# Graph network kernel: the destination tiles of the two convolutions cut into chunks of 2, 3, 3, 3, 3, 3, 4, 4 instead of 1, 3, 3, 3, 3, 4, 4, 4

## The reference

```
xw   = x @ W
norm = rsqrt(deg[src]) * rsqrt(deg[dst])
h    = segment_sum(xw[src] * norm, dst) + b
# first network: batch norm over the nodes, relu, h = x + h
# second: layer norm over the features, silu, then a two-head attention
```

## Time and profile before

| | us |
|---|---|
| median of three runs | 3359.72 |
| lowest, highest | 3355.37, 3362.70 |
| profiled execution, own time | 3363.56 |
| its span, first to last instruction | 3361.9 |
| first convolution, first to last matmul | 298.1 to 379.8 |
| second convolution, first matmul to last sums copied | 419.0 to 515.6 |

### The profile page before, as it was taken

The page is one execution under the profiler, slowest core; times in us unless marked ns, Lnnn a source line. Parts: engine busy times, 40 slices in busy tenths (PEclk is TensorE's granted clock), DMA queues, the critical chain, the costliest instruction groups (busy, mean ns, idle before and its releaser), DMA issues. The chain is left out here.

```text
span 3361.9 us, 41194 instructions
## 1 busy us (share of the span) xinstructions
PE 2803.2 (83%) x13998; PEld 2153.0 (64%) x13998; DVE 1752.6 (52%) x4008; ACT 1368.4 (41%) x2596; POOL 965.7 (29%) x786
## 2 busy tenths in 40 slices
PE   6778797999996999999999999999744455447997
PEld 3446684777774778778887877786433344435775
DVE  8997657999977351121111112112544443356994
ACT  4573134999996121111111111111413333342896
POOL 6110070000000643223222322220177777740000
PEclk9998897999998999999999999999855555555999
DMA  4434352111002432212121212210242221113200
GB/s 151 144 105 157 137 200 88 40 40 77 8 1 92 162 117 88 79 59 98 59 94 68 88 64 98 85 64 5 87 129 47 46 55 29 29 19 128 79 35 20
DMA packets 79695, 266.66 MB, mean 79 GB/s; under 512 B 21129, under 2 KB 53344, under 8 KB 70176
## 3 DMA queue, kind: packets, MB, share of 16 engines
q1 hardware_dynamic: 62520, 236.50, 18.9%
q0 software_dynamic: 16976, 27.54, 3.8%
HBM read 232.80 MB, written 31.18 MB: 79 GB/s over the span
## 5 line engine op out<-in xcount | busy, mean ns | idle before, releaser
L2798 PE MATMUL psum<-gate_stream,parts 128*128 128x384 f32 (+1 forms) x3600 | 668.8, 344 | 15.9 <-POOL gate_stream L2871 11.6
L2798 PEld LDWEIGHTS psum<-gate_stream,parts 128*128 128x128 f32 x3600 | 632.4, 189 | 32.9 <-issue 13.4
L2871 POOL CAST gate_stream<-gate_adj 128x1920 fp32r<-128x1920 f16 (+1 forms) x200 | 370.6, 1860 | 851.9 <-PE psum L2798 829.7
L2150 PE MATMUL psum<-gat_h,gat_pair 128*128 128x129 f32 (+1 forms) x3750 | 571.9, 292 | 8.6 <-DVE gat_pair L1954 7.8
L2150 PEld LDWEIGHTS psum<-gat_h,gat_pair 128*128 128x128 f32 (+1 forms) x3750 | 462.4, 191 | 123.3 <-issue 77.9
L1482 POOL DMA_INDIRECT edge_rows<-edge_table,src_idx x440 | 429.8, 977 | 181.4 <-issue 133.8
L2889 DVE SCALAR_TENSOR_TENSOR gate_work<-psum,bhh,gate_work 128x384 f32<-128x384 f32 (+1 forms) x80 | 50.0, 626 | 793.7 <-PE psum L2761 763.1
L1954 DVE SCALAR_TENSOR_TENSOR gat_pair<-gat_above,gat_adj 128x512 f32<-128x512 f32 (+3 forms) x525 | 326.4, 622 | 87.7 <-PE psum L2150 58.7
L2063 ACT ACTIVATE gat_above<-psum,gat_as 128x512 f32<-128x512 f32 (+3 forms) x525 | 329.4, 627 | 42.7 <-PE psum L2138 41.0
L2054 ACT ACTIVATE psum<-gat_ad_rows,gat_as 128x512 f32<-128x512 f32 (+3 forms) x525 | 334.9, 638 | 16.8
L1909 DVE SCALAR_TENSOR_TENSOR gat_acc<-gat_adj,gat_q,gat_acc 128x512 f32<-128x512 f16 (+3 forms) x497 | 328.3, 677 | 0.0
(11 more groups left out here) (484 smaller groups left out, 3700.1 us busy)
## 6 DMA issues: line engine op xcount, KB each, us to landing
gate_adj<-adj SPq DMA_DIRECT2D x35, 2400.0 KB, 8.1
gat_adj<-adj SPq DMA_DIRECT2D x8, 3200.0 KB, 10.8
adj<-count_stage SPq DMA_DIRECT2D x196, 100.0 KB, 1.7
gcn_adj<-adj SPq DMA_DIRECT2D x8, 2400.0 KB, 8.1
edge_place<-row_scratch SPq DMA_DIRECT2D x40, 352.0 KB, 3.6
gate_adj<-adj SPq DMA_DIRECT2D x5, 2800.0 KB, 9.0
gcn_adj<-adj SPq DMA_DIRECT2D x4, 3200.0 KB, 10.0
edge_rows<-edge_table,src_idx POOLq DMA_INDIRECT x440
```

The costliest lines, as they stand in the source:

```text
L2150: mm = e.matmul(ps[0:p, b, a:a + D + 1], pair[:, g % 2, i * P:i * P + p], h1[:, hi, h, :], start=hi == 0 and i % 3 == 0, stop=hi == NT - 1 ...
L2798: mm = e.matmul(ps[:, f, 0:hi - lo], parts[:, t, m, f, :], stream[:, (NGG * i + t // GG) % GR, 0:windows(i), t % GG * W:(t % GG + 1) * W], ...
L2871: e.tensor_copy(stream[:, n % GR, 0:windows(i), :], cols[:, i % 2, 0:windows(i), g * GW:(g + 1) * GW]).then_inc(widened, 1)
```

## The change

The list of tiles is changed, and with it the table that says at which of the last counting steps VectorE adds the identities of chunks 0 and 1, which are now five tiles in place of four. The chunk widths go from 128, 384, 384, 384, 384, 512, 512, 448 to 256, 384, 384, 384, 384, 384, 512, 448.

```diff
-GCN_TILES = (1, 3, 3, 3, 3, 4, 4, 4)
+GCN_TILES = (2, 3, 3, 3, 3, 3, 4, 4)
...
-        own_at = {BSTEPS - 1: (0, 0), BSTEPS - 2: (1, 0), BSTEPS - 3: (1, 1), BSTEPS - 4: (1, 2)}
+        own_at = {BSTEPS - 1: (0, 1), BSTEPS - 2: (0, 0), BSTEPS - 3: (1, 2), BSTEPS - 4: (1, 1), BSTEPS - 5: (1, 0)}
```

## The result

The kernel with chunks of 2, 3, 3, 3, 3, 3, 4, 4 took 3353.64 us (median of 18 runs, 3347.85 to 3363.21), and the kernel before, run beside it, 3358.61 (18 runs, 3353.5 to 3364.2). The ratio is 0.9985, with a 95% interval of 0.9978 to 0.9992: 5.0 us shorter, between 2.7 and 7.4. The profiled execution took 3350.91 us, span 3349.3, mean granted clock 0.875 (before 0.87).

The account below looks back on a forecast made before the run. The prediction took TensorE to bound the first convolution and a loop over four engines the second, from chunk 2 on. Terms of -2.4 and -1.5 us sum to -3.9, forecasting 3356.0 us, range 3351.5 to 3361.5.

Parts of the forecast that it names:

- "same" by the bound of 0.2%: Whole kernel: a change within about 0.2% (6.7 us) counts as no change; chance 0.79, faster 0.17, slower 0.04.
- Chunk 5: First convolution: 384 columns in place of 512 at full clock, 11.67 to 8.76 us, 2.91 us gained.
- Chunk 0 and the clock: First convolution: chunk 0 of 256 columns 0.3 us longer at 11.25; clock rises 0.33 us later, at 313.85.
- The pace of 256 columns at 1.2 GHz: Chunk 0's matmuls: 256 / 1.2 + 12 = 225 ns each, bounded by 217 to 219 and 331 ns.
- The slower rival: Chunk 0 runs near 331 ns a matmul, weight load only partly hidden: +1.9 us, 3361.7; chance 0.10.
- The first cast: First convolution: casting 1280 elements takes 0.82 us against 489 ns for 640, so TensorE starts 0.33 us later.
- The columns of chunk 2: First convolution: eleven small loads stand ahead in SyncE's queue, so chunk 0's later casts do not delay this load.
- signs named for "wrong": Chunk 0 over 14 us, TensorE idle between first-convolution chunks, 384 turns over 12 us, or over 1 us change outside the convolutions.
- the start predicted at +0.65: Second convolution: a first cast of 1.9 us makes TensorE start at about 419.65 in place of 419.01.
- The loop: Second convolution, first casts of chunks 3 to 7: 48.13 us in place of 51.43, 3.30 us gained.
- The shift before it: Second convolution: chunk 3's first cast comes 1.4 to 2.1 us later than 448.36, taken as 1.8.
- The rival of a larger gain: Chunk 0 keeps 217 ns at both starts, second convolution starts only 0.7 late: -5.2 us, 3354.5; chance 0.17.

Follow-up runs that it names:

- a1_first_only: New tiles in the first convolution only, against the kernel before with bounded register values (3741.39 us): 3737.44 us; first convolution 75.7 us against 80.6.
- a2_second_only: New tiles in the second convolution only, against the kernel before with bounded register values (3741.39 us): 3736.65 us; second convolution 92.9 us against 95.7.
- a3_twice: Old tiles, chunk 0's matmuls stream their 128 columns twice, against the kernel before with bounded register values (3741.39 us): 3735.29 us.
- a5_loads_last: Eleven small loads issued behind chunk 7's load, against the changed kernel with bounded register values (3399.24 us): 3397.42 us; first convolution 73.5 us against 75.6.
- a4_loads_late: Eleven small loads issued behind chunk 2's columns, against the changed kernel with bounded register values (3399.24 us): 3397.19 us; first convolution 77.5 us against 75.6.
- b8_on_act: Second convolution's scaling moved from VectorE to ScalarE, against the changed kernel with bounded register values (3399.24 us): 3406.75 us; second convolution 95.7 us against 92.9.

## Why the prediction was right, and where its steps were wrong

The time, 3353.64, lies in the range, 2.4 us under the predicted 3356.0, and "same" by the bound of 0.2% was right. The sum said -3.9 us and the runs say -5.0. Set against the rows (6.16 us in the two profiles), the steps were:

1. **Chunk 5**, -2.91: 11.75 to 8.86 us, -2.9. Right.
2. **Chunk 0 and the clock**, +0.17 together: wrong. "I let the clock rise that much later too, at 313.85." It rose at 303.3. Chunk 0 took 8.3 us, against 10.9 before and 11.25 in the sum, and chunk 1 lost its slow part, 2.0 us: 4.6 us of gain where the sum had a small loss. I had two rows for the rise, both after 128-column starts, and made of them a time since the first matmul, although also let it be read as a time since the first matmuls wider than 128 columns, at about 309. The runs of a1_first_only, a2_second_only and a3_twice go with that reading and against mine.
3. **The pace of 256 columns at 1.2 GHz**, 225 ns: measured 212 by the same division and 213 from start to start, which is the pace of 81 and 128 columns as well. The 11 ns over the streaming time came from dividing 3.31 us by ten matmuls, where the row counts eleven, those cut by its ends among them; 384 columns take 320 ns from start to start, no more than 384 / 1.2. The slower rival, with 295 ns and more, is refuted.
4. **The first cast**, +0.33: the first matmul came 298.54 - 298.14 = 0.40 later. Right.
5. **The columns of chunk 2**: that the later end of chunk 0's casts "does not delay them" was right (issued at 302.75 and 302.69), but the sum put no price on how long they take behind the small loads, 13.4 us. The price was 2.42 us of idle TensorE. With the clock as I had it the columns were in time; a chunk 0 and 1 that are 4.6 us faster reach them. a5_loads_last shows it: 8.1 us and no pause.
6. The first convolution is thus 0.40 - 2.6 - 2.0 - 2.9 + 2.4 = -4.7 us against -2.4, by the rows 379.77 - 375.18 = 4.59 earlier. Of the signs named for "wrong", an idle TensorE between chunks came, and the block was 76.6 us instead of 79.
7. **Between the convolutions**: from the last matmul of the one to the first of the other 40.51 us instead of 39.24. 0.68 is the start predicted at +0.65 (5.25 against 4.57 us between the product of line 2247 and the first matmul). 0.59 is that product itself, 6.67 us in place of 6.08, with the clock up 1.9 us after its first matmul instead of 0.7: not predicted.
8. **The loop**, 48.13 us for the casts of chunks 3 to 7: 48.11. And 15.30 for the last chunk, which was to stay at 15.31.
9. **The shift before it**, +1.80: from the end of line 2247's product to chunk 3's first cast it is 35.08 us, against 33.91 before, +1.17. It was under the 1.4 to 2.1 named, because the start of the stage gained from the clock as well: by the same measure chunk 1's norm started only 0.11 us later (28.07 us against 27.96), where the sum had 1.2. The rest is its line 1248, which waits for the fifth cast and takes 1.24 us where it took 0.16, as the sum had it. -3.30 + 1.17 is -2.1 instead of -1.5, and chunk 7's first cast came 2.15 us earlier, more than the 1.2 to 1.9 named.

-4.59 + 0.59 - 2.16 = -6.16 us, of which the medians show 5.0 with an interval that holds both. So the number was near in part by luck: two large terms that I had not foreseen, -4.6 from the clock and +2.4 from the loads, partly cancel. The named sign of a difference over 1 us outside the two convolutions came too, 6.4 us in the two profiles; 4.45 of it are the block at the end of the edge stage, and the rest is open. The rival of a larger gain (3354.5) was nearer. Its pace was right (213 ns against its 217), but 8 ns less on 50 matmuls are 0.4 us at each start; what came was the clock.

## What to carry to other kernels

A stage that begins at half clock has a price that depends on its first matmuls: read what TensorE was doing when the clock rose, and not only when, before a time of it is moved. A stage made faster reaches its next wait, so the loads behind a gain are to be checked with the gain in, and small ones kept out of the queue ahead of the large. Where GpSimd and VectorE take turns, count the turn as casts plus what can only follow them, and move that to an engine which can work during the casts.

## What the runs showed of the hardware

- Behind a quiet stretch the clock was up 3.1 to 6.2 us after the first matmul where this kernel's float32r streams began with 256 or 384 columns (22 starts), and after 13.6 to 15.4 where they began with 128 (6 starts). The product of line 2247, also 128 columns wide, has it 0.7 and 1.9 us after its first, close behind transposes. Why these differ stays open.
- In the first convolution TensorE paused once for 1.9 to 2.6 us at full clock in nine of the executions. In three the clock fell (2.19, 2.48 and 2.55 us), in six it did not (2.58 among them). A fall cost the 384-column chunks 1.5 us in a4_loads_late and b8_on_act.
- The same 54 matmuls at the end of the edge stage ran in about 11.6 or 7.2 us, eight and six times in 14 profiled executions, with no edit that goes with it.
- From start to start these float32r matmuls, each with its weight load, take 213 ns at 1.2 GHz for 81, 128 or 256 columns and 320 for 384; at 2.4 GHz 111 for 128, 118 for 256, 175 for 384 and 233 for 512.
- The first 2400 KB that the first convolution loads (chunk 2's) landed 8.1 or 8.2 us after their issue in the three executions with no small loads ahead of them, and 11.7 to 13.4 us in the eleven behind the small loads.
- On three values VectorE's shift (line 1248 of the kernel) takes 0.16 us without casts beside it and 1.24 with them; the reciprocal, with one input, takes 0.17 or 0.18 with and without them.
